# A gated cross-attention block with a slot memory on one Trainium2 core: the features of each block of 512 are laid out in pairs

## The reference

```
K      = ctx @ Wk.T + bk                      # 64 keys per batch
Q      = LN(x) @ Wq.T + bq
attn   = softmax(Q @ K.T / sqrt(2048))
x      = x + tanh(g_xattn) * attn @ ctx
h      = LN(x)
query  = h @ fWq.T                            # 64 wide
scores = (query @ Wr.T) @ (aux_keys @ Wr.T).T / sqrt(48) + log_rel
w      = softmax over the 8 best slots of query @ aux_keys.T / 8 + log_rel
aux    = (w @ aux_values) @ Wvd.T @ Wvu.T
u      = from var(h) and gelu(h @ Wu1.T + bu1) @ Wu2.T + bu2, clipped
out    = x + tanh(g_ffn) * (h + gate(u) * aux)
```

## Time and profile before

| | us |
|---|---|
| median of 3 runs | 1071.44 (1069.85 to 1072.76) |
| profiled execution | 1074.47 |
| its span, first to last instruction | 1072.6 |
| TensorE busy | 1041.0 (97%) |
| VectorE busy | 791.6 (74%) |
| ScalarE busy | 561.6 (52%) |
| GpSimd busy | 183.4 (17%) |

### The profile page before, as it was taken

One profiled execution on the slowest core, in us unless ns is written; L12 is line 12 of the kernel. 1 busy time (PEld: TensorE's weight loads), 2 busy tenths in 40 slices (PEclk: granted clock), 3 DMA queues, 4 the chain that ended last, 5 costly groups with the idle time before them and its releaser, 6 DMA issues. The chain is left out here.

```text
span 1072.6 us, 19294 instructions
## 1 busy us (share of the span) xinstructions
PE 1041.0 (97%) x6778; PEld 997.1 (93%) x6778; DVE 791.6 (74%) x1841; ACT 561.6 (52%) x881; POOL 183.4 (17%) x355
## 2 busy tenths in 40 slices
PE   6998999999999999999999999999999996999997
PEld 6998999998999999999999999999999995888885
DVE  4889646366758787787777787786877777788785
ACT  3643678544635545454554545454554554555553
POOL 0007000000002222313232222312232231000000
PEclk9999899999999999999999999999999997999999
DMA  8555557689379864744354734347352527999999
GB/s 241 157 155 193 196 212 291 246 295 280 94 219 242 218 176 117 214 110 125 92 142 115 196 98 123 112 112 214 98 142 79 151 62 228 402 409 412 403 422 371
DMA packets 109617, 218.96 MB, mean 204 GB/s; under 512 B 48388, under 2 KB 64804, under 8 KB 95528
## 3 DMA queue, kind: packets, MB, share of 16 engines
q1 hardware_dynamic: 99784, 180.68, 55.8%
q10 hardware_dynamic: 9216, 33.56, 7.9%
q0 software_dynamic: 576, 4.19, 0.9%
HBM read 174.10 MB, written 54.79 MB: 213 GB/s over the span
## 5 line engine op out<-in xcount | busy, mean ns | idle before, releaser
L56 PE MATMUL tk_bank<-b_weights,k_turned 128*128 128x384 f32 (+2 forms) x1056 | 348.8, 330 | 1.5 <-DVE b_weights L889 1.4
L58 PE MATMUL tk_bank<-b_weights,k_turned 128*128 128x384 f32 (+2 forms) x1056 | 339.9, 322 | 0.0
L57 PE MATMUL tk_bank<-b_weights,k_turned 128*128 128x384 f32 (+2 forms) x1056 | 339.7, 322 | 0.0
L56 PEld LDWEIGHTS tk_bank<-b_weights,k_turned 128*128 128x128 f32 x1056 | 198.6, 188 | 4.7 <-DVE b_weights L889 1.6
L57 PEld LDWEIGHTS tk_bank<-b_weights,k_turned 128*128 128x128 f32 x1056 | 198.8, 188 | 1.3
L58 PEld LDWEIGHTS tk_bank<-b_weights,k_turned 128*128 128x128 f32 x1056 | 198.3, 188 | 0.0
L1487 DVE STREAM_TRANSPOSE tk_bank<-k_rows 128x512 f32<-128x512 f32 x128 | 133.7, 1069 | 9.1 <-DMA k_rows<-in_x_dram 8.9
L1273 ACT ACTIVATE k_turned<-tk_bank 128x512 fp32r<-128x512 f32 x124 | 71.2, 594 | 73.9 <-DVE tk_bank L1487 73.5
L1897 DVE TENSOR_TENSOR late_x<-late_x,ob_out 128x512 f32<-128x512 f32 x96 | 65.8, 688 | 24.0 <-PE ob_out L58 22.6
L1497 DVE TENSOR_TENSOR k_turned<-tk_bank,k_turned 128x512 fp32r<-128x512 f32 x124 | 79.8, 686 | 0.9
L56 PE MATMUL tk_bank<-k_turned,a_T 128*128 128x256 f32 x256 | 76.1, 297 | 4.4 <-DVE a_T L343 3.9
(11 more groups left out here) (259 smaller groups left out, 2262.0 us busy)
## 6 DMA issues: line engine op xcount, KB each, us to landing
k_rows<-in_x_dram SPq DMA_DIRECT2D x40, 1024.0 KB, 4.8
k_rows<-in_x_dram SPq DMA_DIRECT2D x128, 256.0 KB, 5.2
late_x<-in_x_dram SPq DMA_DIRECT2D x24, 1024.0 KB, 8.3
out_dram<-late_x ACTq DMA_DIRECT2D x48, 512.0 KB, 14.1
k_rows<-in_Wq_dram SPq DMA_DIRECT2D x16, 1024.0 KB, 4.9
k_rows<-in_Wk_dram SPq DMA_DIRECT2D x9, 1024.0 KB, 4.8
out_dram<-k_rows ACTq DMA_DIRECT2D x16, 512.0 KB, 11.4
k_rows<-in_Wk_dram SPq DMA_DIRECT2D x28, 256.0 KB, 5.3
```

The costliest lines, as they stand in the source:

```text
L56: pe.matmul(out, lh, rh, start=start, stop=False, skip_group_check=skip)
L57: pe.matmul(out, lh, rl, start=False, stop=False, skip_group_check=skip)
L58: return pe.matmul(out, ll, rh, start=False, stop=stop, skip_group_check=skip)
```

## The change

A chunk of features is no longer every 16th feature of all 2048. The features are taken in blocks of 512; each block gives four chunks, and a chunk takes every second feature of one half of the block (`features`: 128 features, two apart, from a start that depends on the chunk). Three things change with it:

- `transpose_group` with `spread=True` reads its source at a step of 2 elements.
- The block DMAs of Wk and x write pieces of 64 elements (256 bytes) in place of 512 elements (2048 bytes): the same bytes in 1024 pieces per DMA, for 128.
- VectorE's turns read two elements apart (`block_order`), and write the bank in one run as before (`turned_order`).

In the score weights the stationary operand's columns are now picked with the step of 2, where chunk c was 128 neighbouring columns, and in return the store of M to scratch writes four chunks of a feature in one run of 4 KB, for four pieces of 1 KB. No instruction is added, dropped or moved on any engine.

```diff
+def features(c):
+    first = QN * (c // 4) + 2 * P * (c % 2) + (c % 4) // 2
+    return slice(first, first + 2 * P - 1, 2)
+
+def block_order(tile, g):
+    return tile.rearrange("p (g m i r) -> p g r m i", g=GROUPS, m=8, i=LANES)[:, g]
+
+def turned_order(bank):
+    return bank.rearrange("p (r m j) -> p r m j", r=2, j=LANES)
@@ transpose_group
-        part = slice(c, D, KC) if spread else slice(c * P, (c + 1) * P)
+        part = features(c) if spread else slice(c * P, (c + 1) * P)
@@ keys_stage
-    wk_blocks = io["Wk"].rearrange("(t k j) (q f) -> t q j k f", k=P // LANES, j=LANES, q=QUADS)
+    wk_blocks = io["Wk"].rearrange("(t k j) (g q f) -> t q j g k f", k=P // LANES, j=LANES, q=QUADS, f=2 * LANES)
-            sp.dma_start(tile[q * LANES:(q + 1) * LANES, :].rearrange("j (k f) -> j k f", f=QN),
+            sp.dma_start(tile[q * LANES:(q + 1) * LANES, :].rearrange("j (g k f) -> j g k f", k=P // LANES, f=2 * LANES),
-            dve.transpose(bank[g][:].rearrange("p (c k j) -> p c k j", c=4, j=LANES),
-                          tile[:].rearrange("p (k i c) -> p c k i", k=P // LANES, c=KC)[:, 4 * g:4 * g + 4]
-                          ).then_inc(block_turned, 1)
+            dve.transpose(turned_order(bank[g][:]), block_order(tile[:], g)).then_inc(block_turned, 1)
@@ score_weights_stage
-                sp.dma_start(scr["mt"][part].rearrange("(c p) n -> p c n", p=P)[:, 4 * k:4 * k + 4, :],
+                sp.dma_start(scr["mt"][part].rearrange("(p c) n -> p c n", c=KC)[:, 4 * k:4 * k + 4, :],
-            hi, lo = T[u]
+            hi, lo = (t[:].rearrange("p c x -> p (c x)") for t in T[u])
-                                    (hi[:, c, :], lo[:, c, :]),
+                                    (hi[:, features(c)], lo[:, features(c)]),
@@ load_blocks, and turn_x of the token stage: the same two edits for x
-    view = io["x"].rearrange("(t k j) (q f) -> t q j k f", k=P // LANES, j=LANES, q=QUADS)
+    view = io["x"].rearrange("(t k j) (g q f) -> t q j g k f", k=P // LANES, j=LANES, q=QUADS, f=2 * LANES)
-                dve.transpose(bank[g % 2][:].rearrange("p (c k j) -> p c k j", c=4, j=LANES),
-                              blocks[:].rearrange("p (k i c) -> p c k i", k=P // LANES, c=KC)[:, 4 * g:4 * g + 4]
-                              ).then_inc(S["turned"], 1)
+                dve.transpose(turned_order(bank[g % 2][:]), block_order(blocks[:], g)).then_inc(S["turned"], 1)
```

More of the change, by code:

```diff
@@ L937, in load_blocks @@
 def load_blocks(sp, io, keep, t):
-    view = io["x"].rearrange("(t k j) (q f) -> t q j k f", k=P // LANES, j=LANES, q=QUADS)
+    view = io["x"].rearrange("(t k j) (g q f) -> t q j g k f", k=P // LANES, j=LANES, q=QUADS, f=2 * LANES)
     for q in range(QUADS):
-        sp.dma_start(keep["blocks"][q * LANES:(q + 1) * LANES, :].rearrange("j (k f) -> j k f", f=QN),
-                     view[bass.ds(t, 1), q].rearrange("o j k f -> (o j) k f")).then_inc(keep["blocks_in"], 16)
+        sp.dma_start(keep["blocks"][q * LANES:(q + 1) * LANES, :].rearrange("j (g k f) -> j g k f", k=P // LANES,
+                                                                            f=2 * LANES),
+                     view[bass.ds(t, 1), q].rearrange("o j g k f -> (o j) g k f")).then_inc(keep["blocks_in"], 16)
 def load_rows(sp, io, keep, t):
```

## The result

The changed kernel takes 1073.9 us (median of 20 runs, 1071.4 to 1077.7); the kernel before, on the same chips, 1070.7 us (20 runs, 1068.4 to 1072.8). The ratio is 1.0032, with a 95% interval of 1.0024 to 1.0040: 3.4 us slower (2.6 to 4.3). I had forecast 1068.0 us, with 1073.0 us as the upper end. Lines of the changed file lie some 14 to 16 further down: L284 is L300, L137 is L153, L87 is L103, L1487 is L1502.

What follows compares the result with a forecast made beforehand. TensorE was taken as the bound. Stall -1.8, TensorE's turns -1.2, stationary operand 0 and DMA 0 gave -3.0 us; with the 0.42 us wait -3.4, from a median of 1071.44 to 1068.0 us, range 1062.5 to 1073.0.

Steps and rivals of the forecast that it cites:

- What bounds the kernel: TensorE, busy for 589.70 of 590.00 us in the token stage; VectorE or DMA gains there are worth nothing.
- VectorE's turns: VectorE's 32x32 turns of 128x512 fall from 1069 to 686 ns; 49 us less in the token stage, worth nothing there.
- DMA, cost 0: Smaller pieces of the block loads land one to two microseconds later per tile, within the slack: cost 0.
- rival of late blocks: Token stage: a tile's blocks land too late; 1074 us at twice the present time, 1146 at three times; chance 0.09.
- The stall, -1.8 us: Keys stage: TensorE's idle behind L284, held beside GpSimd's centring, shrinks from 3.5 to 2.4 us, plus 0.7 of slow clock.
- the second half of the train: Keys stage: the second eight of GpSimd's sixteen centring TENSOR_TENSORs; L284 arrives 1.1 us inside and waits until they end.
- rival of full relief: Keys stage: L284 arrives before the second half or slips between its instructions; 7.9 us go, 1063.5 us; chance 0.19.
- TensorE's turns, -1.2 us: 64 groups of four strided transposes get faster at step 2, between 0 and 1.9 us; 1.2 taken.
- The stationary operand, 0: Score weights: 768 loads of the centred Wq at step 2 stay hidden beside the matmuls; 0, upper bound 5.8 us.
- The wait of 0.42 us at 29.92: TensorE's wait for VectorE's L343 in the first body, with two turns in front of it, goes: -0.42 us.

Runs made afterwards that it cites:

- e4: The changed kernel with Wk's block loads back in 2048-byte pieces, x's still in 256-byte pieces: 1070.01 us, ratio 1.0000 to the kernel before.
- e2: The changed kernel with both block loads, Wk and x, back in 2048-byte pieces, turns and reads as changed: 1070.89 us, ratio 1.0002 to the kernel before.
- e1: The changed kernel with the seven small loads issued ahead of the first four Wk block loads: 1070.42 us, ratio 1.0001 to the kernel before.
- e3: The changed kernel with x's block loads back in 2048-byte pieces, Wk's still in 256-byte pieces: 1075.09 us, ratio 1.0048 to the kernel before.
- e17: The kernel before, all pieces large, with its seven small loads moved behind the wait ahead of the second Wk blocks: 1074.43 us, ratio 1.0032.
- e9: The kernel before with TensorE's reads at a step of 2 and GpSimd's sixteen centring instructions cut to 4 of 256 columns: 1071.26 us, ratio 0.9993.
- e7: The kernel before with only TensorE's reads changed, to a step of 2: 1077.62 us in two groups of runs, ratio 1.0052.
- e18: e12 with the row tiles of Wk from tile 3 on issued by ScalarE: 1072.59 us, ratio 1.0021 to the kernel before.
- e15: The changed kernel with the row tile ahead of the second Wk blocks, the small loads left late: 1072.09 us, ratio 1.0006 to the kernel before.
- e8: The kernel before with the 64 strided groups of TensorE's transposes reading 128 neighbouring elements: 1069.25 us, ratio 0.9980.
- e16: The changed kernel with both block loads in pieces of 512 bytes, 512 a DMA: 1070.57 us, ratio 0.9992 to the kernel before.
- e12: The changed kernel with chunks of 128 neighbouring features, block loads in 128-byte pieces and small loads first: 1074.97 us, ratio 1.0033 to the kernel before.

## Why the prediction was wrong

**What bounds the kernel**: right. TensorE is busy for all of the token stage, and 45 us less on VectorE, or blocks in other pieces (e4), move nothing there.

**VectorE's turns**: right. 709 ns for a forecast 686, and together with the reads worth nothing that can be told (e2).

**DMA, cost 0**: this is the step that failed. "SP holds no other work between the block loads and the row load that it issues 4 us later, so a queue that fills costs nothing either. In the keys stage the blocks are issued a whole body ahead." The first sentence is right for the token stage; the second answers when the blocks are needed, not who stands behind them on SP. I priced the landing of the moved bytes (and there 256-byte pieces cost nothing: the blocks of x landed sooner, where I took one to two microseconds later) and not SP's issue, and gave no row of SP before 514 us. The loads behind the Wk blocks, which TensorE needs at 25.7 and 34.9 us, were issued 3 to 13 us later, since four block loads held SP for 15.08 us where they had held it for 2.47: +3.4 us (e1, e3, e17). A row of the kernel before could have warned, a load of 512 KB in 2048 pieces of 256 bytes:

```profile
243.29 4.76 SPq L994 DMA_DIRECT2D b_weights<-scratch_centred  x1
```

My rival of late blocks, with 0.09 of the chances, had the price of its small end, 1074 us, but put it in the token stage, at the batch starts. That the time came out there is luck: the blocks were not late.

**The stall, -1.8 us**: the size was wrong for the timed runs, since it came from one execution. The profiled run lay 3 us over the median, which I noted and subtracted at the end, and did not ask which of the waits in it was that difference. The step that failed here is the reading that the second half of the train does not let L284 in: it came where I put it, and was let in (e1, 1.50 us). With GpSimd's train cut the time of the kernel before changes by 0.0 us (-1.3 to +1.2), so 1.8 us could not be had. In the profiled run of the changed kernel it was gone whole (my rival of full relief), and that is why the two profiles stand the wrong way round: 6.3 us of stall less, 3.0 us of start-up waits more. By these the difference would be 3.3 us; it is 1.1. Of the rest, 1.5 us lie ahead of 17 us: TensorE began at 8.88 us, when the context had landed, for 7.88 before, and then waited 0.88 us for rows of Wk, for 0.35. That is from execution to execution and not from the pieces: TensorE began at 7.88 us in e9 and 8.90 in e7, with large pieces, and at 7.87 in e18 and 9.13 in e15, with small ones.

**TensorE's turns, -1.2 us**: wrong in its reason. "Less than 0 I exclude, since step 2 lies between the two": the weight loads take 209 ns at step 2, 196 at step 16 and 141 at step 1, and a group's pace has the same order (0.40, 0.38 and 0.35 us). The bound for neighbouring elements was good (e8), but step 2 is not near it. The times alone are less sharp: e9 puts the reads' part at -0.7 us, -1.9 to +0.5, and e2, with the turns, at +0.2, -0.9 to +1.3.

**The stationary operand, 0**: right. The score weights are as dense as before (901 matmuls in 107.97 us; 895 before, with a clock of 0.99).

**The wait of 0.42 us at 29.92** went, as said, inside the start-up that cost more.

With the start-up waits out of the way, what is left of the forecast -3.4 us is nothing: e1's ratio is 1.0001, 0.9990 to 1.0011.

## What to carry to other kernels

When a DMA's pieces get smaller, list what stands behind it on the queue that issues it, with the time at which each of these is needed, above all at the start where the queue is full of large loads; issue small loads that somebody waits for ahead of loads in many pieces. Before a stall is priced from a profile, compare the profiled execution with the timed runs: one that lies above them all (here by 1.7 us over the slowest) may have a stall that most runs have not, and a version with the stall's cause taken away tells. A layout that frees an engine which is not the bound is worth what it does to the engine that is, here nothing.

## What the runs showed of the hardware

- Where the block loads had 128 pieces, SP's issue of a DMA took 0.3 to 2.2 us in the first 50 us, and of a block load up to 3.3 us in the token stage (e2). In the first 50 us it took, with 512 pieces, 6.8 us for the third block load in a row (e16); with 1024, up to 12.4 us for the third (e3), behind the loads of the context and two row tiles; with 2048, 8.2 us for the second (e12).
- Loads of 256 KB into 32 partitions landed in 5.2 us at the median in pieces of 2048 bytes, 4.5 us in pieces of 256 bytes and 4.8 us in pieces of 128 bytes.
- The 32x32 turn of 128x512 takes 1067 to 1070 ns when it reads at a step of 64 bytes, and 708 to 709 ns at 8 bytes as at 4.
- TensorE's weight loads for fp32 transposes are not ordered by their step: 141 ns at 4 bytes (e8, e12), 209 at 8 (e7), 196 at 64.
- VectorE's 128x256 TENSOR_TENSOR with two SBUF inputs takes 0.42 us alone and 0.7 to 1.5 us beside GpSimd's train of TENSOR_TENSORs, and took 8.70 us once, in one of 16 profiled executions.
